# Second layer's attention: normalisation statistics from VectorE to ScalarE, and three reorderings of the loop's instruction streams

## The reference, cut to what matters

```python
h = _layernorm(x, axis=-1) * (1 + ca) + sa
x = x + ga * _L1_attn_ref(h, ...)        # linear attention with softplus features
h = _layernorm(x, axis=-1) * (1 + cb) + sb   # the "second norm"
x = x + gb * _L1_ffn_ref(h, ...)         # mixture of 8 experts, the best 2 for each token

def _layernorm(x, axis=-1, eps=1e-05):
    m = jnp.mean(x, axis=axis, keepdims=True)
    v = jnp.var(x, axis=axis, keepdims=True)
    return (x - m) / jnp.sqrt(v + eps)

# attention: q = softplus(x@Wq.T + bq), k = softplus(x@Wk.T + bk), v = x@Wv.T + bv
kv = cumsum(k[..., :, None] * v[..., None, :]);  k1 = cumsum(k)
out = (q @ kv) / sum(q * k1);  out @ Wo.T + bo
# experts: logits = t @ gate_w + gate_b;  top_v, top_i = top_k(logits, 2)
```

## Time and profile before

| | us |
|---|---|
| median of 3 runs | 938.74 (937.11 to 945.42) |
| the profiled execution's own time | 945.22 |
| its span, first to last instruction | 943.4 |
| TensorE busy | 858.5 (91%) |
| VectorE busy | 774.1 (82%) |
| ScalarE busy | 618.2 (66%) |
| GpSimd busy | 566.4 (60%) |

### The profile page before, as it was taken

One profiled execution on the slowest core, in us unless ns is written; L12 is line 12 of the kernel. 1 busy time (PEld: TensorE's weight loads), 2 busy tenths in 40 slices (PEclk: granted clock), 3 DMA queues, 4 the chain that ended last, 5 costly groups with the idle time before them and its releaser, 6 DMA issues.

```text
span 943.4 us, 24125 instructions
## 1 busy us (share of the span) xinstructions
PE 858.5 (91%) x7676; PEld 674.7 (72%) x7692; DVE 774.1 (82%) x2369; ACT 618.2 (66%) x1603; POOL 566.4 (60%) x547
## 2 busy tenths in 40 slices
PE   6979898998999989999999999999879999999990
PEld 5945576645445458888778877787668888888890
DVE  3988787999999736988999999999886866666996
ACT  3557123487888446467677777666557888888880
POOL 1211004277776414443888888888777777777773
PEclk9989999899999999999999999999998999999996
DMA  5330262233223203001111112111227766756987
GB/s 155 95 95 1 67 204 59 104 110 141 102 101 130 99 3 96 15 17 35 43 52 49 49 54 64 53 50 49 66 68 219 219 183 183 228 181 196 338 263 248
DMA packets 93962, 105.82 MB, mean 112 GB/s; under 512 B 16095, under 2 KB 75802, under 8 KB 91661
## 3 DMA queue, kind: packets, MB, share of 16 engines
q1 hardware_dynamic: 81884, 84.59, 29.3%
q0 software_dynamic: 8640, 17.97, 5.3%
q10 hardware_dynamic: 3312, 1.70, 0.6%
HBM read 79.91 MB, written 24.32 MB: 110 GB/s over the span
## 4 chain that ended last, share of the span: by engine, by line
PE 48%; DVE 8%; issue 2%; ACT 2%; DMA 2%; POOL 1%; SPq 0%; ACTq 0%; DVEq 0%; POOLq 0%
PE ps L2694 12%; PE ps L2450 10%; PE ps L2717 6%; PE ps L2466 2%; PE ps L2513 2%; PE ps L2441 2%; PE ps L2416 2%; PE ps L2677 2%; PE ps L2567 2%; PE ps L2551 2%; PE ps L2429 1%; DVE qk L2001 1%; DVE qk L2007 1%; PE ps L2461 1%; DMA parts<-gx,dest 1%
## 5 line engine op out<-in xcount | busy, mean ns | idle before, releaser
L1641 POOL TENSOR_TENSOR kvb<-qk,v 128x1024 f32<-128x1024 f32 x64 | 127.3, 1995 | 68.8 <-DVE qk L2007 48.9
L1650 POOL DMA_INDIRECT rows_of<-payb,posu x128 | 144.3, 1128 | 40.1 <-issue 27.5
L2450 PE MATMUL ps<-con,kvb 128*128 128x128 f32 x1024 | 126.0, 276 | 0.0
L1161 PE MATMUL ps<-masked,ew 128*128 128x512 f32 x256 | 123.3, 610 | 1.9 <-DVE masked L1091 1.8
L2450 PEld LDWEIGHTS ps<-con,kvb 128*128 128x128 f32 x1024 | 119.4, 192 | 1.0 <-issue 1.0
L2378 DVE TENSOR_SCALAR qk<-ps,b 128x256 f32<-128x256 f32 x142 | 62.1, 478 | 49.7 <-PE ps L2694 44.6
L1674 POOL DMA_INDIRECT parts<-h,dest x72 | 80.6, 1119 | 23.3 <-issue 20.1
L1674 POOL DMA_INDIRECT parts<-gx,dest x70 | 78.7, 1125 | 21.3 <-issue 19.2
L1091 DVE TENSOR_TENSOR masked<-f_t,wide 128x512 f32<-128x512 f32 x128 | 85.9, 715 | 4.9 <-PE ps L1161 4.7
L1983 DVE TENSOR_TENSOR qc<-ps,qk 128x1024 f32<-128x1024 f32 x64 | 78.0, 1218 | 9.3 <-PE ps L2450 8.2
L1161 PEld LDWEIGHTS ps<-masked,ew 128*128 128x128 f32 x256 | 44.8, 192 | 44.9 <-issue 30.0
(11 more groups left out here) (370 smaller groups left out, 2107.0 us busy)
## 6 DMA issues: line engine op xcount, KB each, us to landing
wide<-hot_dram SPq DMA_DIRECT2D x16, 1024.0 KB, 4.6
kvb<-rows_of SPq DMA_DIRECT2D x71, 132.0 KB, 2.5
ex<-in_w_dram SPq DMA_DIRECT2D x36, 256.0 KB
lg<-in_w_dram SPq DMA_DIRECT2D x35, 256.0 KB
toep<-taps_dram SPq DMA_DIRECT2D x16, 512.0 KB, 4.5
xg<-parts SPq DMA_DIRECT2D x16, 512.0 KB, 5.2
x_tok<-in_x_dram SPq DMA_DIRECT2D x16, 256.0 KB, 2.9
rb<-den_dram SPq DMA_DIRECT2D x64, 64.0 KB
```

Of the source, the lines that this page charges most:

```text
L1161: nc.tensor.matmul(ps[:, w % 2, :], ew0[:, e, :], masked[e % 4][:, :], start=False, stop=(e == E - 1)).then_inc(s["product"], 1)
L1641: nc.gpsimd.tensor_tensor(kv[g % KB][:, :, :].rearrange("p e (h d) -> p e h d", h=H), k_in, v_in, ALU.mult).then_inc(s["kv"], 1)
L1650: nc.gpsimd.indirect_dma_start(rows_of, bass.IndirectOffsetOnAxis(ap=posu[w % PR][:, slot, t:t + 1], axis=0), pay[w % PB][:, t, :], None). ...
L2450: last = nc.tensor.matmul(cum(g)[:, e, :], kv[g % KB][:, e, :], k("upto"), start=True, stop=True)
```

## The change

VectorE's `moments` is gone. ScalarE gets three new steps for the same sequence: `row_sums` (four copies with an accumulated sum), `negative_means` (one small operation) and `centred_squares` (four squares with the negative mean as bias, with an accumulated sum); they are issued between `payload` and `turned_pay`. `variance_log` waits for the last of them. VectorE's `shifted` multiplies the negative mean with the root. In VectorE's list `corrected` and `softplus` come ahead of `logits`; `residual` stands between `logits` and `largest`; `shifted` and `gated` come ahead of `ranked` and `placed`. In TensorE's list `ranks` comes behind the last `sums`.

```diff
+            sx = sb("sx", [P, C], scope=sc)
+            nm = [sb(f"nm{j}", [P, C], scope=sc) for j in range(2)]
+            vs = [sb(f"vs{j}", [P, C], scope=sc) for j in range(2)]
+            unread = sb("unread", [P, C, D], scope=sc)
...
+                    def row_sums(w):
+                        if exists(w):
+                            need(act, "x3", w + 1)
+                            need(act, "nm", w)
+                            need(act, "vs", w)
+                            for c in range(C):
+                                last = nc.scalar.activation(unread[:, c, :], tile(w, c), ACT.Copy, accum_out=sx[:, c:c + 1])
+                            last.then_inc(s["sx"], 1)
+
+                    def negative_means(w):
+                        if exists(w):
+                            need(act, "sx", w + 1)
+                            need(act, "vs", w - 1)
+                            need(act, "sh", w - 1)
+                            nc.scalar.activation(nm[w % 2][:, :], sx[:, :], ACT.Copy, scale=-1.0 / D).then_inc(s["nm"], 1)
+
+                    def centred_squares(w):
+                        if exists(w):
+                            need(act, "nm", w + 1)
+                            need(act, "lv", w - 1)
+                            for c in range(C):
+                                last = nc.scalar.activation(unread[:, c, :], tile(w, c), ACT.Square, bias=nm[w % 2][:, c:c + 1], accum_out=vs[w % 2][:, c:c + 1])
+                            last.then_inc(s["vs"], 1)
...
-                            need(act, "mv", w + 1)
+                            need(act, "vs", w + 1)
...
-                            nc.scalar.activation(rv[w % 2][:, :], mv[w % 2][:, :, 1], ACT.Ln, bias=eps[:, :]).then_inc(s["lv"], 1)
+                            nc.scalar.activation(rv[w % 2][:, :], vs[w % 2][:, :], ACT.Ln, bias=eps[:, :], scale=1.0 / D).then_inc(s["lv"], 1)
...
                         payload(n - 7)
+                        row_sums(n - 5)
+                        negative_means(n - 5)
+                        centred_squares(n - 5)
                         turned_pay(n - 7)
...
-                    def moments(w):
...
-                            nc.vector.scalar_tensor_tensor(sh[w % 2][:, :], mv[w % 2][:, :, 0], -1.0, rv[w % 2][:, :], ALU.mult, ALU.mult).then_inc(s["sh"], 1)
+                            nc.vector.tensor_tensor(sh[w % 2][:, :], nm[w % 2][:, :], rv[w % 2][:, :], ALU.mult).then_inc(s["sh"], 1)
...
                         weighted(n - 1, 1)
+                        corrected(n)
+                        softplus(n)
                         logits(n - 5)
+                        residual(n - 2)
                         largest(n - 5)
                         chosen(n - 5)
-                        corrected(n)
-                        softplus(n)
-                        residual(n - 2)
                         weighted(n - 1, 2)
                         states(n)
+                        shifted(n - 3)
+                        gated(n - 4)
                         ranked(n - 5)
                         placed(n - 5)
-                        shifted(n - 3)
-                        gated(n - 4)
                         weighted(n - 1, 3)
-                        moments(n - 2)
                         first_cum(n)
...
                         bridge_tail(n, B + 2, (2, 9, 10, 9))
+                        sums(n - 2, 3)
                         ranks(n - 6)
-                        sums(n - 2, 3)
                         bridge_tail(n, B + 2, (2, 3, 3))
                         turn_pay(n - 5)
```

More of the change, by code:

```diff
@@ L1298, in build @@
             rows = [sb(f"rows{u}", [P, 3, D], scope=sc) for u in range(W)]
-            st = sb("st", [P, C, 6], scope=sc)
-            mv = [sb(f"mv{j}", [P, C, 2], scope=sc) for j in range(2)]
+            sx = sb("sx", [P, C], scope=sc)
+            nm = [sb(f"nm{j}", [P, C], scope=sc) for j in range(2)]
+            vs = [sb(f"vs{j}", [P, C], scope=sc) for j in range(2)]
+            unread = sb("unread", [P, C, D], scope=sc)
             ms = [sb(f"ms{j}", [P, C], scope=sc) for j in range(2)]
@@ L1347, in build @@
                      "exp", "u1", "cor", "sub", "ln", "qk", "kv", "tri", "qc", "red", "k1", "qd", "st_ps", "ds", "skv", "den", "rden", "den_out", "spread0", "spread1",
-                     "att", "fold_ps", "fold", "folded", "wo", "wo_t", "wo_ps", "x3", "st", "mv", "lv", "rs", "sh", "me", "rm", "normed", "cb", "h4", "sq",
+                     "att", "fold_ps", "fold", "folded", "wo", "wo_t", "wo_ps", "x3", "sx", "nm", "vs", "lv", "rs", "sh", "me", "rm", "normed", "cb", "h4", "sq",
                      "pay", "pay_ps", "pay_t", "gx", "x4", "lg_ps", "lg_t", "lg_back", "lg", "max", "idx", "idf", "hot", "ed", "ee", "e1", "p1", "taken", "counted", "carried",
```

## The result

The changed kernel takes 994.43 us (median of 4 runs, 990.92 to 1003.58) against 941.29 us for the kernel before in the same comparison: ratio 1.058, 95% interval 1.054 to 1.062. It is slower by 53 us where I had predicted 27 (966, range 955 to 980). The sign and the wait that carries it came as predicted; the size is double.

The account below looks back on a forecast made before the run. TensorE and VectorE were both nearly full, bound by waits between them. A new loop from `back` over `ranked` and `turn_pay` would add 21.3 + 2.3 + 3.4 = 27 us to 938.74, giving 966 us, range 955 to 980.

Parts of the forecast that it names:

- the chain of terms: Full iteration: 5.57 us from `back` to `turn_pay` plus 16.71 to the next `back`, 22.28 us, +1.94 an iteration.
- Alone this is worth up to 0.90 us an iteration: `corrected` and `softplus` ahead of the choice: TensorE's stop before `states` goes, a gain of up to 0.90 us an iteration.
- the later `send`: GpSimd's `send` gets its addresses 2.4 us later, TensorE itself is 1.94 later; GpSimd's idle time covers the rest, cost 0.
- the part on which I put the result: `residual` ahead of `largest` and `chosen`: VectorE waits for `back`, closing a loop through `ranked` and `turn_pay`, +1.94 us an iteration.
- the loop should keep 2.4 GHz: TensorE, busy about 19 of 22.3 us (85%) in a full iteration, keeps its full clock there.
- VectorE's 5.57 us: VectorE's steps from the end of `back` through `ranked` to the start of `turn_pay`, summed to 5.57 us.
- `ranks` behind the sums: TensorE's `ranks` moved behind the last `sums`: `turn_pay` comes behind both anyway, so cost 0.
- TensorE's own work: Rival: `ranked` ends before TensorE finishes the last `sums`, only the 0.90 us gain remains, 929 us; chance 0.06.
- the order that does not bind: Rival: the new wait for `ranked` is only about the 0.90 us it replaces, 930 to 947 us; chance 0.05.
- ScalarE's loop: Rival: ScalarE's eight operations take 5.0 us instead of 3.5, 1.3 us more an iteration, 980 us; chance 0.07.
- The clock: Iterations 17 and 18: TensorE may fall to 1.2 GHz earlier, 4 to 8 us more, 970 to 974; 0.35 within the forecast.
- The statistics: Statistics moved from VectorE to ScalarE: about 3.5 us there, off the path on both engines, cost 0 by a thin margin.

Follow-up runs that it names:

- the kernel with small products and spare matmuls: Changed kernel with GpSimd's products cut to an eighth of their elements and 3 + 9 unread matmuls in TensorE's stop, iterations 5 to 15: 967.18 us.
- the one with the counts moved: Kernel before with the four operations from the one-hot table on behind the softplus, `ranked` directly behind `residual`, GpSimd's order as before: 966.17 us, ratio 1.0264.
- with the clock held: Changed kernel with 3 unread matmuls ahead of `ranks` and 9 between `ranks` and `turn_pay`, iterations 5 to 15: 988.18 us, ratio 1.0516.
- the run alone: Kernel before with the statistics on ScalarE and none of the three reorderings: 943.71 us, ratio 1.0015.
- the kernel with both moves: Changed kernel with 3 + 9 unread matmuls in TensorE's stop and the subtraction of the two largest logits behind the index search: 982.97 us, ratio 1.0459.

## Why the prediction was half right

**Right: the wait.** `turn_pay` waits 2.41 us for `ranked` (2.5 to 3 predicted), `residual` up to 1.7 for `back` (1 to 2), `weigh` 3.2 (2 to 3), and the stop at `states` is gone. The loop is back, VectorE, `ranked`, `turn_pay`, TensorE, as in the chain of terms, and the kernel with small products and spare matmuls shows that its terms add up: 22.22 us where I had 22.28.

**Wrong: "Alone this is worth up to 0.90 us an iteration".** Softplus first, alone, costs 41 us. I followed the softplus to TensorE and not to GpSimd, though the list of who needs it, in the kernel before in words, has `products`. GpSimd waited for the softplus before; two rows of the kernel before that I had not read, GpSimd's in the iteration of the earlier trace rows and VectorE's in iteration 16, hold what was needed:

```profile
591.15 1.96 POOL L1641 TENSOR_TENSOR kvb<-qk,v 128x1024 f32<-128x1024 f32 x1 [0.52 <-DVE qk L2007]
```

```profile
665.66 1.25 DVE L2090 TENSOR_TENSOR wts<-top 128x4 f32<-128x4 f32 x1
```

The first says that a product of 2 us cannot start before the softplus. Beside it VectorE did `residual`, `weighted` and `states`, each with one operand in PSUM, and these do not stall. With the softplus first, nothing keeps the product off the choice, which has small operations with both operands in SBUF, and these do stall. The second row is such a stall, 1.25 us in place of 0.25, under a product from 664.89 to 666.87.

Where the product then falls is set by GpSimd's sends and no longer by the softplus. Their addresses come late (the wait for `posu` is 48.4 us in all, before 10.3), and the product follows a `send`, 0.84 us behind the softplus in the changed kernel and 2.17 with the softplus alone moved. The prediction put the later `send` at 0: TensorE waits for GpSimd nowhere in that window, but the choice meets the product. An estimate from the rows after: started 0.08 us behind the softplus, as before, the product would have ended at 590.64 + 0.08 + 1.99 = 592.71, where the subtraction starts. No run shows that.

**Half wrong: "the part on which I put the result".** The wait of `residual` for `back` is in the trace, and with port and clock out of the way the loop that it closes still costs 24.7 us (967.18 against 942.49), near the 27 of the forecast. But in the changed kernel, with `residual` behind the choice again, the time is the same, 994.86. Its place is one way to the loss; the softplus's place is what all of the slow kernels have in common, apart from the one with the counts moved, which puts some of the same operations under the same product. No run has `residual` ahead of the choice and the softplus behind it.

**Wrong: "the loop should keep 2.4 GHz".** This is the step of the sum that failed most: a cost in each full iteration that it put at nothing. I argued from TensorE's busy share, 85% of the iteration, which came out right (20.77 of 24.30). The granted clock fell all the same and is 0.50 in the first 2.34 us of the iteration, so `turn_pay`, `first_cum` and `queries` take 573.46 to 577.15, 3.69 us, against 573.61 to 575.80, 2.19, before. That is +1.50 of the 2.02 us by which the iteration missed. The mean over an iteration did not tell it. The clock fell towards the end of the second of two stops, 0.96 and 2.41 us with two tiny matmuls between; with spare matmuls in them it stayed at 1.00. The Trainium skill (TensorE: Matmul & The Clock Gate, "What's actually happening") has the low clock as the default that activity lifts; the trace agrees, and I had applied that to the tail only.

**Mis-sized: VectorE's 5.57 us.** This is the other step of the sum that failed: 6.10 measured (591.66 to 597.76). `largest` and `chosen`, priced at 2.38, take 2.89 (592.30 to 595.19), with the subtraction under the product. Small in this kernel, where the subtraction starts 1.22 us behind the product's start; with the clock held it starts 0.12 ahead of it, and the chain is 1.9 us too long.

**The other terms.** Eleven full iterations, 427.94 to 695.97, take 268.0 us, before (431.22 to 654.96) 223.7: +44.3 (21.3 predicted). The tail, from iteration 15's `turn_pay` to the last choice, +7.2 (5.7 predicted), the clock there 0.72 to 0.85 in three of the four 5 us windows from 730 to 750, which I had as the upper end. From the end of the first softplus to the first `turn_pay` +0.7 (71.8 against 71.1). Together +52.2, near the 53.1 by which the medians differ. The profiled executions differ by 47.4, as that of before was 4.0 us later already at its first softplus (360.14 against 356.18), where nothing of the change has run; between the profiled executions of this case that point lies from 353.9 to 366.1. Behind the last choice both are as long, 240.6 and 240.0 us, as predicted. `ranks` behind the sums: 0 was wrong alone (+6 us).

**The rivals.** None took the forecast's place. TensorE's own work and the order that does not bind fell with the wait of 2.41 us, ScalarE's loop with `p_t`, below. The clock, which I had priced at 4 to 8 us in the last iterations, cost 1.50 in each of the full ones, some 16 us.

**The statistics: right.** 0 by the run alone. The eight operations and the small one take 571.47 to about 574.6, 3.1 us (3.5 estimated from the earlier trace rows), and `p_t` follows without a wait, where it waited 4.00 us in the earlier trace rows. ScalarE's timeline after, one row of each kind:

```profile
571.47 0.29 ACT L1694 ACTIVATE unread<-x_tok 128x128 f32<-128x128 f32 x1
...
572.76 0.21 ACT L1702 ACTIVATE nm<-sx 128x4 f32<-128x4 f32 x1
573.00 0.40 ACT L1709 ACTIVATE unread<-x_tok,nm 128x128 f32<-128x128 f32 x1
...
574.61 0.60 ACT L1860 ACTIVATE p_t<-ps 128x512 f32<-128x512 f32 x1
```

**Open.** What softplus-first would give with neither port nor clock in the way was not run. From its rows, 6.88 less 2.50 for the table and 1.30 for the slow sums is 3.08 us from `back` to `turn_pay`, against 3.63 before: an estimate of some 0.5 us an iteration to be won, if the choice could be kept clear of the product.

## What to carry to other kernels

Before an operation is moved forward, ask for each of its readers what that reader will start and when, and on VectorE beside GpSimd's products look at where the operands of the neighbours lie: in these runs what reads one operand from PSUM passes, and what reads two from SBUF stands until the product is over, however small it is. A wait that is added in a loop can cost twice, as the wait and as the clock behind it; read the clock right behind the stop, not the mean of the iteration. Where two such costs overlap, take both away in one kernel: singly they gave 6 and 9 us, together 27.

## What the runs showed of the hardware

VectorE's operations beside GpSimd's 128x1024 product, in the kernel after, medians without and with an overlap: additions of two SBUF operands of 128x512 (L2075), 0.69 and 2.64 us; the 128x4 subtraction 0.17 and 0.62, at most 1.99; with one operand in PSUM, 1.223 and 1.217 (128x1024) and 0.687 and 0.689 (128x512); the four largest-of-eight 0.15 each in both cases. The rows above show the stalled operation ending with the product or up to its own length behind it, so it does not share, it waits. The Trainium skill (SBUF — State Buffer, "SBUF: two separate sides") calls the port pair of VectorE and GpSimd an exclusive lock held for the whole instruction, against VectorE's operations with two SBUF inputs; the trace agrees on both. By that section whichever starts first has the pair; by the records the one-hot table started 0.66 us ahead of the product (585.08 and 585.74) and yet waited for all of it, so the order of recorded starts does not tell who waits. A cast with one input stood for 1.66 us too (the kernel with both moves); the section also names VectorE's operations in a two-port performance mode, and whether the cast is one no run shows. A VectorE row's time holds this wait and no idle time shows it: a mean above the smallest of the same shape is the sign to look for.
